# Two graph layers on one core: rows of a tile 64 apart, TensorE's transposes ahead of the contraction, and a wait ahead of the first gathers

## The reference

```
deg = sum(adj, axis=1);  x1 = (adj @ x) / deg
x   = layernorm(x + concat[x1, x] @ weight + bias)
h   = x @ W.T;  e = (h @ a1)[:, None] + (h @ a2)[None, :];  e = where(adj == 0, -inf, e)
out = layernorm(x + softmax(e, axis=1) @ h)
```

## Time and profile before

| | |
|---|---|
| median of 3 runs | 1146.62 us (1145.8 to 1148.38) |
| profiled execution, its own time | 1149.24 us |
| its span in the profile | 1147.6 us |
| TensorE busy | 1010.7 us (88%), 8777 matmuls |
| VectorE, ScalarE, GpSimd busy | 715.9, 607.5, 321.2 us |
| mean granted clock of TensorE | 0.976 of full speed |
| moved by DMA | 305.36 MB, of which 268.45 MB by the gathers |

### The profile page before, as it was taken

How to read it: one execution, slowest core, us unless ns; L and a number is a source line. 1 busy time by engine, 2 the same in 40 slices (tenths; PEclk the granted TensorE clock), 3 DMA queues, 4 the chain that set the end, 5 groups by cost and what they waited for, 6 DMA issues and landing times.

```text
span 1147.6 us, 22057 instructions
## 1 busy us (share of the span) xinstructions
PE 1010.7 (88%) x8777; PEld 874.9 (76%) x8777; DVE 715.9 (62%) x1722; ACT 607.5 (53%) x531; POOL 321.2 (28%) x333
## 2 busy tenths in 40 slices
PE   0278777787989989899999999999999999999997
PEld 0157655676878778787888888888888888888886
DVE  2488866687766766676576655555553665656554
ACT  1667767777868667767776676666541110000000
POOL 2344434434444343343433433333200000000000
PEclk9999988989999989999999999999999999999999
DMA  9799988999999999899989879787903022211211
GB/s 280 230 378 402 418 325 350 372 361 371 380 357 398 362 363 362 338 376 332 352 337 346 339 287 364 272 343 284 356 6 114 10 80 79 78 45 46 69 50 30
DMA packets 51594, 305.36 MB, mean 266 GB/s; under 512 B 6560, under 2 KB 7840, under 8 KB 17952
## 3 DMA queue, kind: packets, MB, share of 16 engines
q0 software_dynamic: 36864, 268.45, 61.3%
q1 hardware_dynamic: 13824, 35.16, 9.4%
q10 hardware_dynamic: 800, 0.30, 0.1%
HBM read 286.29 MB, written 17.59 MB: 265 GB/s over the span
## 4 chain that ended last, share of the span: by engine, by line
PE 78%; DVE 10%; issue 5%; DMA 3%; ACT 2%; SPq 1%; DVEq 0%; ACTq 0%
PE ps_agg L313 50%; PE ps_part L313 20%; PE ps_y L313 4%; DVE edgesT L742 3%; DMA x_all<-in_x_dram 3%; DVE edgesT L741 2%; DVE stray L751 1%; PE ps_y L590 1%; PE ps_y L589 1%; ACT L477 1%; PE ps_h L597 1%; DVE stats L792 1%; SPq L348 1%; DVE z L788 1%; DVE x_big L856 1%
## 5 line engine op out<-in xcount | busy, mean ns | idle before, releaser
L313 PE MATMUL ps_agg<-parts,edgesT 128*128 128x257 f16 (+1 forms) x5312 | 641.4, 279 | 118.5 <-DVE edgesT L742 118.5
L313 PEld LDWEIGHTS ps_agg<-parts,edgesT 128*128 128x128 fp8e4 x5312 | 527.5, 100 | 211.8 <-DVE edgesT L742 127.6
L451 ACT ACTIVATE edges<-adj_in 128x4096 fp8e4<-128x4096 int32 x128 | 462.0, 3611 | 7.8 <-DVE edgesT L742 3.8
L1130 POOL DMA_INDIRECT adj_in<-in_adj_dram,chunk x256 | 289.8, 1132 | 443.2 <-ACT edges L451 401.1
L313 PE MATMUL ps_part<-parts,edgesT 128*128 128x258 f16 x1664 | 194.6, 273 | 0.0
L313 PEld LDWEIGHTS ps_part<-parts,edgesT 128*128 128x128 fp8e4 x1664 | 162.7, 98 | 22.8
L751 DVE SCALAR_TENSOR_TENSOR stray<-edgesT,stray 128x1024 uint32<-128x1024 uint32 x128 | 156.6, 1223 | 0.1
L516 ACT ACTIVATE std<-mean_var,eps 128x1 f32<-128x1 f32 x64 | 18.9, 295 | 204.0 <-DVE mean_var L962 204.0
L457 ACT ACTIVATE catT<-ps_catT 128x256 f32<-128x256 f32 x64 | 24.6, 384 | 176.9 <-PE ps_catT L579 174.9
L313 PE MATMUL ps_part<-parts,packed 128*128 128x258 f16 x836 | 96.3, 273 | 0.0
L741 DVE STREAM_TRANSPOSE edgesT<-edges 128x512 uint32<-128x512 uint32 x128 | 89.4, 698 | 3.7 <-ACT edges L451 3.4
(11 more groups left out here) (99 smaller groups left out, 677.0 us busy)
## 6 DMA issues: line engine op xcount, KB each, us to landing
x_all<-in_x_dram SPq DMA_DIRECT2D x16, 256.0 KB, 28.2
adj_in<-in_adj_dram,chunk POOLq DMA_INDIRECT x256
out_dram<-edges SPq DMA_DIRECT2D x60, 64.0 KB, 2.9
partial_sums<-partial SPq DMA_DIRECT2D x13, 258.0 KB
adj_in<-partial_sums SPq DMA_DIRECT2D x13, 258.0 KB, 6.1
packed_adj<-packed SPq DMA_DIRECT2D x3, 1024.0 KB
adj_in<-packed_adj SPq DMA_DIRECT2D x2, 1024.0 KB, 6.2
packed<-packed_adj SPq DMA_DIRECT2D x1, 1024.0 KB
```

What stands on the lines that cost most here:

```text
L313: done = eng.matmul(bank[:, 0:cols], rows[:, n // BYTES, n % BYTES, :], moving[:, n, :], start=(n == first), stop=(n == last))
L451: act.activation(edges[:, half, :, :], adj_in[:, n % SLOTS, :, :], ACT.Copy, scale=2.0 if t % GROUP == GROUP - 1 else 1.0, saturate=False) ...
L1130: pool.indirect_dma_start(adj_in[:, n % SLOTS, r, :], None, adj_chunks, bass.IndirectOffsetOnAxis(chunk[:, 0:1], 0), element_offset=first_ ...
```

## The change

Which rows make a tile: partition p = 32 a + w now stands for the 64 consecutive rows 64 p to 64 p + 63 of x, h and the output, and tile t is the rows 64 p + t. (Before, tile t = 4 g + c was the rows 2048 a + 128 g + 4 w + c.) So x is loaded in four DMAs of 1 MB, 8 KB in a row for each partition, the output of a group is one DMA over 128 partitions, and the last tile's rows are one DMA on SyncE instead of two each on SyncE and ScalarE. The rows of `adj` in one gather are 64 apart instead of four. VectorE's transposes read words that are 16 words apart instead of adjacent ones.

Where operations stand: TensorE does `transpose_cat(t - 1)` and `transpose_x1(t - 3)` ahead of the whole contraction of t, and `hidden` has a lag of three tiles instead of two. ScalarE's step is the copies, then `weighted_hi`, the first conversion, `deviation`, `weights`, the second conversion, and `copy_h`. On VectorE `weighted` stands behind the moments, `exponents` and `weighted_lo` behind the second half's transposes, and `normed` at the step's end. The group's exponents come one tile later. The order of the last tiles' pieces in the second layer follows from it.

GpSimd waits for the second x load to land before its first gather.

```diff
-    x_quarters = x.rearrange("(a s b w c) f -> s a w b (c f)", a=NQ, s=QUARTERS, b=NB // QUARTERS, w=QUAD, c=BYTES)
-    out_groups = out.rearrange("(a g w c) f -> g a w c f", a=NQ, w=QUAD, c=BYTES)
+    x_blocks = x.rearrange("(p n) f -> p n f", n=NBLK)
+    out_groups = out.rearrange("(p g c) f -> g p c f", g=GROUPS, c=GROUP)
...
         def exponents_at(g):
-            return GROUP * g + 6 if g > 0 else 8
+            return GROUP * g + 7 if g > 0 else 9
...
-        def weighted_lo_at(g):
-            return exponents_at(g) + 2
...
             for s in range(QUARTERS):
-                for a in range(NQ):
-                    sp.dma_start(x_all[QUAD * a:QUAD * (a + 1), QBLK * s:QBLK * (s + 1), :]
-                                 .rearrange("p (b c) f -> p b (c f)", c=BYTES), x_quarters[s, a]).then_inc(s_x[s], 16)
+                blk = slice(QBLK * s, QBLK * (s + 1))
+                sp.dma_start(x_all[:, blk, :], x_blocks[:, blk, :]).then_inc(s_x[s], 16)
...
-                for r in range(NQ):
-                    sp.dma_start(out_groups[loads[j], r], y_out[QUAD * r:QUAD * (r + 1), j % 4, :, :])\
-                        .then_inc(s_outst[j % 4], 16)
+                sp.dma_start(out_groups[loads[j]], y_out[:, j % 4, :, :]).then_inc(s_outst[j % 4], 16)
...
-            for t in range(TILES + 2):
+            for t in range(TILES + 3):
+                if on(t, 1):
+                    copy_catT(t - 1)
+                if on(t, 3):
+                    copy_x1T(t - 3)
+                for g in range(GROUPS - 1):
+                    if t == weighted_at(g):
+                        weighted_hi(g)
+                if on(t + 1, 0):
+                    convert(t + 1, 0)
                 if on(t, 2):
                     deviation(t - 2)
-                if on(t + 1, 0):
-                    convert(t + 1, 0)
-                if on(t, 1):
-                    copy_catT(t - 1)
-                if on(t, 2):
-                    copy_x1T(t - 2)
-                if on(t + 1, 0):
-                    convert(t + 1, 1)
-                if on(t, 2):
-                    copy_h(t - 2)
                 for g in range(GROUPS - 1):
                     if t == exponents_at(g):
                         weights(g)
-                    if t == weighted_at(g):
-                        weighted_hi(g)
+                if on(t + 1, 0):
+                    convert(t + 1, 1)
+                if on(t, 3):
+                    copy_h(t - 3)
...
             for t in range(TILES):
-                first_layer(t, range(0, NBLK // 2))
                 if on(t, 1):
                     transpose_cat(t - 1)
-                if on(t, 2):
-                    transpose_x1(t - 2)
-                first_layer(t, range(NBLK // 2, NBLK))
+                if on(t, 3):
+                    transpose_x1(t - 3)
+                first_layer(t)
                 if on(t, 1):
                     project(t - 1)
-                if on(t, 2):
-                    hidden(t - 2)
+                if on(t, 3):
+                    hidden(t - 3)
...
-                src = edges[:, half, :, :].bitcast(u32).rearrange("p r (b w) -> p r b w", b=NB)
+                src = edges[:, half, :, :].bitcast(u32).rearrange("p r (w b) -> p r b w", b=NB)
...
             def step(t):
-                for g in range(GROUPS - 1):
-                    if t == weighted_at(g):
-                        weighted(g)
...
                 if on(t, 2):
                     moments_joined(t - 2)
-                if t == 8:
+                for g in range(GROUPS - 1):
+                    if t == weighted_at(g):
+                        weighted(g)
+                if on(t, 0):
+                    transpose_half(t, 1)
+                if t == 9:
                     keep_shift()
                 for g in range(GROUPS - 1):
                     if t == exponents_at(g):
                         exponents(g)
-                if on(t, 0):
-                    transpose_half(t, 1)
-                if on(t, 2):
-                    normed(t - 2)
-                for g in range(GROUPS - 1):
-                    if t == weighted_lo_at(g):
-                        weighted_lo(g)
...
+                for g in range(GROUPS - 1):
+                    if t == weighted_at(g):
+                        weighted_lo(g)
+                if on(t, 2):
+                    normed(t - 2)
...
-                          channel_multiplier=NQ * BYTES).then_inc(s_chunk, 1)
+                          channel_multiplier=NQ * NBLK).then_inc(s_chunk, 1)
...
-                    first_row = JQ * (2 * half + r) + P * g + c
+                    first_row = JQ * (2 * half + r) + t
...
+            pool.wait_ge(s_x[1], 16)
             for n in range(SLOTS):
                 load_half(n)
```

More of the change, by code:

```diff
@@ L332, in exponents_at @@
         def exponents_at(g):
-            return GROUP * g + 6 if g > 0 else 8
+            return GROUP * g + 7 if g > 0 else 9
         def weighted_at(g):
             return exponents_at(g) + 1
-        def weighted_lo_at(g):
-            return exponents_at(g) + 2
-        ALL_STORED = [16 * NQ * sum(1 for j in range(GROUPS - 1) if j % 4 == s) for s in range(4)]
+        ALL_STORED = [16 * sum(1 for j in range(GROUPS - 1) if j % 4 == s) for s in range(4)]
         @block.sync
@@ L400, in _ @@
             sp.wait_ge(s_out, TILES - 1)
-            for r in range(NQ):
-                sp.dma_start(out_groups[loads[j], r, :, 0:GROUP - 1, :],
-                             y_out[QUAD * r:QUAD * (r + 1), j % 4, 0:GROUP - 1, :]).then_inc(s_outl, 16)
+            sp.dma_start(out_groups[loads[j], :, 0:GROUP - 1, :], y_out[:, j % 4, 0:GROUP - 1, :]).then_inc(s_outl, 16)
             sp.wait_ge(s_out, TILES)
-            for r in range(NQ // 2):
-                sp.dma_start(out_groups[loads[j], r, :, GROUP - 1, :],
-                             y_out[QUAD * r:QUAD * (r + 1), j % 4, GROUP - 1, :]).then_inc(s_outl, 16)
+            sp.dma_start(out_groups[loads[j], :, GROUP - 1, :], y_out[:, j % 4, GROUP - 1, :]).then_inc(s_outl, 16)
             for s in range(4):
                 sp.wait_ge(s_outst[s], ALL_STORED[s])
-            sp.wait_ge(s_outl, 16 * 2 * NQ)
+            sp.wait_ge(s_outl, 16 * 2)
             sp.wait_ge(s_flag, 1)
@@ L517, in _ @@
                     .then_inc(s_std1, 1)
[L519 to L522, removed]
             act.wait_ge(s_flag, 1)
@@ L558, in _, with first_layer @@
             pe.matmul(ps_small[:, F:F + 1], w1_sb[:, :], a2_sb[:, :], start=True, stop=True).then_inc(s_w1T, 1)
[L560 to L565, removed]
-                        pe.wait_ge(s_lo0, s + 1)
-                        last = contract(pe, ps_agg[0], edgesT[:, 0, :], parts0[:, :, 0:2 * F + 1],
-                                        range(QBLK * s, QBLK * (s + 1)), 0, NBLK - 1)
-                else:
-                    last = contract(pe, ps_agg[t % 2], edgesT[:, t % 2, :], parts0[:, :, 0:2 * F + 1], blocks,
-                                    0, NBLK - 1)
-                if blocks[-1] == NBLK - 1:
-                    last.then_inc(s_agg, 1)
+            def first_layer(t):
+                pe.wait_ge(s_trh, 2 * t + 2)
+                wait(pe, s_aggr, t - 1)
+                for s in range(QUARTERS):
+                    if t == 0:
+                        pe.wait_ge(s_lo0, s + 1)
+                    last = contract(pe, ps_agg[t % 2], edgesT[:, t % 2, :], parts0[:, :, 0:2 * F + 1],
+                                    range(QBLK * s, QBLK * (s + 1)), 0, NBLK - 1)
+                last.then_inc(s_agg, 1)
             def transpose_cat(t):
@@ L635, in _ @@
             pe.wait_ge(s_aggr, TILES - 1)
-            second_layer(0, range(0, 28))
+            second_layer(0, range(0, 16))
             transpose_cat(TILES - 1)
+            transpose_x1(TILES - 3)
+            second_layer(0, range(16, 36))
+            project(TILES - 1)
+            hidden(TILES - 3)
             transpose_x1(TILES - 2)
-            second_layer(0, range(28, 44))
-            project(TILES - 1)
+            second_layer(0, range(36, READY))
             hidden(TILES - 2)
-            second_layer(0, range(44, 56))
-            pe.wait_ge(s_lo1, GROUPS - 1)
-            second_layer(0, range(56, 60))
-            transpose_x1(TILES - 1)
             pe.wait_ge(s_unp, 2)
             second_layer(1, range(0, 16))
+            transpose_x1(TILES - 1)
+            second_layer(1, range(16, 32))
             hidden(TILES - 1)
-            second_layer(1, range(16, 60))
+            second_layer(1, range(32, READY))
             pe.wait_ge(s_unp, 3)
             pe.wait_ge(s_partk, TILES - EARLY)
-            second_layer(2, range(0, 60))
+            second_layer(2, range(0, READY))
+            pe.wait_ge(s_lo1, GROUPS - 1)
+            for u in range(3):
+                second_layer(u, range(READY, READY + GROUP))
             pe.wait_ge(s_lo1, GROUPS)
             for u in range(3):
-                second_layer(u, range(60, NBLK))
```

(4 more changed lines are left out.)

15 lines of the change are left out of this document (7 added, 8 removed).

## The result

The changed kernel takes a median of 1117.07 us (1107.79 to 1119.09, 4 runs) against 1147.5 for the kernel before; the ratio is 0.9704, with an interval of 0.963 to 0.9778. It is faster, as forecast, and inside the range; the forecast of 1087 us was 30 us too low. Its four runs lie 11 us apart, those of the kernel before 10 us.

What follows compares the result with a forecast made beforehand. Bound by a late start, then a TensorE-VectorE loop with DMA nearly as late, then exp stalls at group borders, with a last stage of pure matmuls; -20 - 26 - 12 - 1 = -59.6 us gives 1087 us, range 1058 to 1130.

Steps and rivals of the forecast that it cites:

- Start, -20 us: Up to tile 3: earlier x loads put the first contraction at 31 us, not 50.4, and tile 3 at 66.5, not 86.7.
- 6.3 MB at 408 GB/s (below) is 15.4 us, 25.7: Start: x's other 2.1 MB and the first two gathered halves (4.2 MB) pass after 10.3 us, landing by 25.7.
- Tiles 3 to 31, -26 us: Early tiles: DMA at 408 GB/s becomes the bound, 10.98 us a tile; 325.4 us in all against 351.7.
- The residue of 1 us a group: Tiles 3 to 31: 1 us left for each of seven groups, for exp, table loads and weighted().
- first rival: Slow transposes: each of four a tile takes 0.63 us more, tiles 3 to 31 take 11.6 us each; 1113 us, chance 0.25.
- the loop of the forecast: Early tiles: TensorE to VectorE and back, 10.48 us less 0.33 of transposes, 10.15 us a tile.
- Tiles 32 to 63, -12 us: Later tiles: TensorE needs 411.4 us and took 426.8; 3 us left for ScalarE's step with exp.
- End, -1 us: Last output store: two issues on SyncE beside two on ScalarE, 2.25 us, become one; -2 to +1 us.
- the likeliest case: Whole kernel: the forecast itself, 1087 us with its own range of 1072 to 1100, chance 0.37.
- The third (the gathers' pitch, slower): Gathers at 2 MB pitch run at 329 GB/s, 13.4 us a tile, over TensorE's need to b = 11; 1178 us, chance 0.14.
- The fourth (the stall stays elsewhere): Group's stall moves to weighted() in mid-step or copy_catT; only start, transposes and tail count; 1122 us, chance 0.08.
- The second (all is hidden): DMA holds 424 GB/s and no group leaves a residue, 22.5 us less than forecast; 1065 us, chance 0.14.

Runs made afterwards that it cites:

- the kernel with both undone: The changed kernel with the gathers' rows 4 apart and transposes of adjacent words, x still in four 1 MB loads: 1077.47 us, ratio 0.9405.

## Why the prediction was right, and where it was off

**What bounds the kernel before** held. The stall at the group's border was the largest thing in it that an experiment removed: moving weighted() alone gave 36.9 us, and the last stage did not move (282.4 and 281.8 us).

**Start, -20 us: -11.9.** Of the 8.2 us by which tile 3 is late (74.75 instead of 66.5), 4.9 lie ahead of the first contraction and 3.4 behind it. Ahead of it two steps failed. "The x conversions are done by about 20 and so hidden": they ended at 26.8, behind weights that land at 18.5, and the two adjacency conversions stood behind them. I had read when x would land and not what ScalarE does ahead of it. And "6.3 MB at 408 GB/s (below) is 15.4 us, 25.7": with the w1T copy moved away, the second half's gathers landed at 28.8 us and were what ended last; the window from 20 to 30 us of the changed kernel moved 340 GB/s. Either delay alone costs some 3 us: the first contraction is at 34.5 with the w1T copy moved away, and at 33.6 to 34.2 in the kernels with faster gathers, where x's conversions still end last. Behind it the three next starts are 38.9 us apart instead of 35.5, and the transposes explain most of that: with adjacent words they are 35.9 apart. What I put down to the wait is not due to it: without the wait the changed kernel takes the same time. It is worth 12.5 and 9.7 us only where x comes in sixteen loads.

**Tiles 3 to 31, -26 us: -9.8.** Three terms were mis-sized. The rate, taken as 408 GB/s: from 90 to 300 us full engines moved 380, and undoing the pitch alone gives 20.5 us in the whole kernel, 13.2 of them in these tiles (341.8 against 328.6). The residue of 1 us a group: at 380 GB/s the forecast's 17.9 MB a group are 29 x 11.78 = 341.5 us, and 341.8 were measured, so nothing was left over for it, and the second error took back 7 us of the first. And the transposes, taken as now: 1.03 us instead of 0.68, a little over half of what the first rival charged (0.35 more, not 0.63). That by itself cost nothing in these tiles, since gathers were the later of the two; with fast gathers it costs 19.1 us. Where both were undone these tiles took 312.4 us, even less than my 325.4, at 410 to 420 GB/s and with the loop of the forecast.

**Tiles 32 to 63, -12 us: -8.0.** TensorE's need, 411.4 us, was right: in the three kernels with gathers at 128 or 512 KB pitch and the new layout these tiles take 411.3 or 411.4 us. In the changed one they take 419.0. So the 3 us left for ScalarE's step with exp were not needed; the gathers cost 7.6 instead, until about 580 us, as its chain shows with a transfer of 14.12 us at 557.90. From 600 us on TensorE has no gap.

**End, -1 us: about -0.6.** As sized.

**Luck.** The measured time lies in the stated range, but outside the 1072 to 1100 of the likeliest case, and near the first rival's 1113 for another reason than that rival gives. The gain's direction and the removed stall were forecast for the right reason; that slower gathers came out inside a range made for slow transposes was luck.

**The rivals.** The first (slow transposes) has the right cause and a little over half the price, and it was not the bound. The third (the gathers' pitch, slower) has the cause that decided: between full rate and its 329 GB/s lay 368 to 383, so the gain shrank and did not turn. The Trainium skill, "DMA: Bandwidth & Descriptors", section Latency and other measured facts, has 207 GB/s for copies at 512 KiB and 164 at 2 MiB, a loss of a fifth; here the gathers fell by a tenth (from 90 to 300 us and with adjacent words in both, 418 GB/s at 128 KB pitch and 373 at 2 MB, at DMA shares of 1.01 and 0.98), with nothing lost at 512 KB. The direction agrees, and that the loss comes above 512 KB; the size is half. The fourth (the stall stays elsewhere) is refuted by 1.1 us of idle time. The second (all is hidden) would have had 306 us in tiles 3 to 31; the kernel with both undone came two thirds of the way there from 325.4, with 312.4.

**Open.** Why 2 MB costs and 512 KB does not is not shown; no run varies the pitch between them, and with the pitch goes the stretch of memory that a gather spans (4, 16 and 64 MB for 32 rows), so the one can't be told from the other. The kernel with the old rows and x loaded 128 partitions at a time was not tried, nor weights issued ahead of x.

## What to carry to other kernels

A change of layout that makes DMAs simpler at one end has two other ends: look at the pitch of the rows that each gather touches, and at the distance of the words that VectorE reads from it. Two limits that run side by side hide each other: the slower transposes were worth nothing or 19 us, by whether the gathers were slow, so undo suspects together as well as one by one. And an instruction that waits at the head of an in-order step is worth moving before anything else: three lines gave 36.9 us where the whole change gave 30.4. Before a step is taken for hidden, read what its engine does ahead of it in its own queue.

## What the runs showed of the hardware that I had not expected

- Gathers of 8 KB runs: rows 128 KB and 512 KB apart gave 1096.6 and 1094.7 us, rows 2 MB apart 1117.1.
- VectorE's 32-bit transposes of 128x512 take 0.68 us (mean of the two instructions) with adjacent words, 1.03 with words 64 bytes apart, 1.10 with words 16 bytes apart in a pattern of one dimension more. The Trainium skill, "SBUF — State Buffer", section Door 1: The DMA port swizzle, asks for two accesses to a 16-byte line for full rate; neither wide pattern has that, and the rows agree that it costs, by a factor of 1.5 to 1.6. That the second is slower than the first does not follow from it.
- Loads of 32 partitions and 256 KB moved 219 to 222 GB/s with full engines, whether their runs were 2 KB or 8 KB.
- Small loads issued beside large ones can land behind them: the last of the weights, issued by 3.2 us, landed at 18.5 us behind 4 MB of x issued by 3.0, and at 11.4 in the kernel with sixteen small x loads and rows 16 apart.
